# The opening of a fused attention-and-experts kernel: where the first bias column, two queries, the bias rows and the first probabilities are computed

## The chip, the cores and the metric

One core of a Trainium2 chip. The metric is the device time of one launch in microseconds (us), lower is better. The kernel before took 1143.11 us, the median of three runs.

## What is computed

Eight sequences of 512 tokens with 512 channels go through a two-way cross-attention with a gate, a residual, and a layer of 8 experts of which each token takes one. Cut to what matters here:

```python
def xattn(char_emb, subword_emb, ...):            # char_emb = layernorm(x), subword_emb = ctx_1024
    Q_char, K_sub, V_sub = linear(char_emb, Wq_c, bq_c), linear(subword_emb, Wk_s, bk_s), linear(subword_emb, Wv_s, bv_s)
    char2sub = softmax(Q_char @ K_sub.T * scale) @ V_sub
    Q_sub, K_char, V_char = linear(subword_emb, Wq_s, bq_s), linear(char_emb, Wk_c, bk_c), linear(char_emb, Wv_c, bv_c)
    sub2char = softmax(Q_sub @ K_char.T * scale) @ V_char
    gate = sigmoid(concat([char2sub, sub2char]) @ Wg.T + bg)
    return gate * char2sub + (1 - gate) * sub2char
x = x + tanh(g_xattn) * xattn(layernorm(x), ctx_1024, ...)
x = x + tanh(g_ffn) * (gate * expert_of_the_token(layernorm(x)))
```

## The kernel before, in words

**Products.** Every 512-wide product is done in two halves of each operand (a rounded high half on fp32r, and the rest): `product` (L155) issues 12 matmuls, 4 chunks of the contraction by 3 pairs of halves. After it ScalarE copies the bank out as the high half (`hi`), and VectorE subtracts that from the bank to give the low half (`lo`). So each 128x512 tile costs a ScalarE and a VectorE instruction, and the tensor engine (PE) waits for `lo`.

**The folded weights.** A query and a key product are replaced by one: for each direction the kernel first computes A = Wq^T Wk. The steps AC and AD (L416, L435 to L438) do that for direction 0, chunk by chunk as the weights come in, into the four banks `u0` to `u3`; AE empties them. A10 to A13 are direction 1. The steps W are the two halves of the raw weights, W00 to W03 of direction 0 and W10 to W13 of direction 1. What the biases add is folded as well: a column of 4x128 numbers Wk^T b that is added to each query (`c_col`, from step FOLD0 for direction 0 and FOLD2 for direction 1), and a row of 512 numbers, with which each token of x or of the context is dotted (`u_row`, from FOLD1 and FOLD2; the dots are the steps XD and CD, L1361 and L1367). SC are VectorE's scaled sums of weight rows (L380) that FOLD1 and FOLD2 read; the sum over the partitions is a matmul with ones.

**Order of the work.** The order is a list of named steps, written by hand, the same list for all five engines; each engine does its own part of each step and skips steps in which it has none. `opening_steps` (L180) is followed by `steps_of_a_batch(True, False)` (L479) for the first sequence, then a hardware loop over sequences 1 to 6, then the last one and the experts. An engine's queue is in order, so an instruction that waits holds up everything behind it in the list. Names end in digits for direction and number (Q02: direction 0, tile 2), or in one digit where there is no direction.

**The steps around the change.** XS (L1343) takes mean and variance of 128 rows of x on VectorE, and GpSimd (L1489) raises the variance to the power -1/2. XN (L1356) normalises the rows; for the first sequence on VectorE, for all later ones on ScalarE (L1211). XT (L1091) transposes them on PE and gives the moving operand of the queries. Q (L1024) is the query product, S (L1038) the scores, NP and S on VectorE the softmax (L1273: reciprocal of the sum, then the rows times it), V the values, PT the transposed probabilities, U the attended values, CT the halves of the context columns, AH and AL the emptying of A10 to A13's banks, WT, WH and WL the halves of the late weights, SM the small scalars, BC the constants of the biases.

**Banks.** `mm0` and `mm1` alternate over the steps Q, V, S and G (`Banks.take`, L793, and `take`, L993); `tr0` and `tr1` take transposes and FOLD1 and FOLD2. FOLD0 writes its column to `mm0`: 4 column tiles by 4 chunks, 16 matmuls with one moving column each, which read the raw fp32 weights and so run as 32 instructions. Queries wait for it:

```python
elif kind == "FOLD":
    if i == 0:
        pe.wait_ge(b_ready, 1)
        for m in range(C):
            for c in range(C):
                last = pe.matmul(column_bank[0][:, m:m + 1], raw[0][1][:, c, m * P:(m + 1) * P],
                                 column(0, 1, c), start=c == 0, stop=c == C - 1)
```

The order of the opening is:

```python
names = """WARM0 W00 AC00 W01 AC01 XS0 W02 XS1 XN0 XS2 W03 AC02 XN1 B0 XS3 XT0 XN2 AC03 XT1 XN3 AE00 AD03
           XT2 XT3 FOLD0 AE01 AE02 AE03 W10 BC0"""
```

GpSimd fills a constant (`fill_i`, L342) in its part of step FOLD2, without a wait. The split of the router's weights in three bf16 parts (L358) belongs to FOLD1 on VectorE.

Of the kernel before, what the change touches and what calls it, by code (L numbers as in the profile page):

```python
# [73 lines left out]
def gated_attention_and_experts(nc, x, ctx_in, g_xattn, g_ffn, Wq_c, bq_c, Wk_s, bk_s, bv_s,  # L74
# [10 lines left out]
    with ExitStack() as top:  # L85
# [26 lines left out]
        k.x1_tile = sb("x1_tile", [P, 2, H])  # L112
        k.junk = sb("junk", [P, H], BF16)
# [63 lines left out]
WEIGHTS_STEPS = ("WARM", "B", "BC", "W", "SC", "AC", "AD", "A", "AE", "AH", "AL", "FOLD", "SM")  # L177
# [14 lines left out]
def weights_part(nc, top, k, x1_dram, list_dram, w):  # L192
# [3 lines left out]
    column_bank = (k.mm_bank[0], k.tr_bank[1], k.tr_bank[1])  # L196
# [15 lines left out]
    in_parts = on_desk(3 * C * E).rearrange("p (n c e) -> p n c e", n=3, c=C)  # L212
# [16 lines left out]
    folded_up = sem("folded_up")  # L229
# [34 lines left out]
    def scalar(act):  # L264
# [7 lines left out]
        def run(step):  # L272
# [15 lines left out]
            elif kind == "SM":  # L288
                act.wait_ge(small_loaded, SMALL)
                act.activation(k.tanh_g[:], g_raw, ACT.Tanh).then_inc(scalars_ready, 1)  # L290
            elif kind in ("AE", "AH"):
                evicted[0] += 1
                if d == 1 and i == 0:
                    act.wait_ge(fold_read, 3)
                    act.wait_ge(router_split, 2 * PARTS - 1)
                act.wait_ge(group_mm, evicted[0])
                act.activation(arena[:, A_X + d, HI, i], bank[i][:], ACT.Copy).then_inc(group_hi, 1)
# [11 lines left out]
    def gpsimd(pool):  # L309
# [29 lines left out]
        def run(step):  # L339
            kind, _, d, c = step  # L340
            if kind == "FOLD" and c == 2:
# [7 lines left out]
    def vector(dve):  # L349
# [19 lines left out]
        def run(step):  # L369
            kind, _, d, i = step  # L370
            if kind == "BC":
# [4 lines left out]
                then(dve.reduce_sum(b_const, product_of, axis=AX))  # L376
            elif kind == "SM":
# [16 lines left out]
            elif kind == "FOLD":  # L394
                dve.wait_ge(fold_mm, i + 1)
                if i != 1:
                    ins = dve.tensor_copy(k.c_col[:, i // 2], column_bank[i][:, 0:C])
# [3 lines left out]
                if i != 0:  # L401
                    dve.tensor_scalar(k.u_const[:, i - 1:i], column_bank[i][:, C:C + 1], SCALE, None, ALU.mult)
                    ins = dve.tensor_copy(k.u_row[:, i - 1], row_bank[:])
                ins.then_inc(fold_read, 1)
                dve.wait_ge(fold_read, i + 1)
                if i == 1:
                    split_router()
# [7 lines left out]
    def tensor(pe):  # L415
# [13 lines left out]
        def run(step):  # L429
# [9 lines left out]
            elif kind == "A":  # L439
                if i == 0:  # L440
                    pe.wait_ge(nat_lo, 16)
                    pe.wait_ge(group_lo, C)
                product(pe, bank[i][:], lambda a, c: pair[1][0][:, a, c, i * P:(i + 1) * P],
                        lambda b, c: pair[1][1][:, b, c]).then_inc(group_mm, 1)
# [34 lines left out]
def steps_of_a_batch(first, last):  # L479
# [38 lines left out]
    s += late(4) + cur("U", 0, 0) + prev("BS", 3) + cur("PT", 0, 1) + opened("CD1")  # L518
# [69 lines left out]
def attention_part(nc, scope, top, k, x_rows, c_rows, x_columns, ctx_columns, x1_dram, x1_early, list_dram, expert_w,  # L588
# [6 lines left out]
    junk, bn_x, mv_x, x1_tile = k.junk, k.bn_x, k.mv_x, k.x1_tile  # L595

# [11 lines left out]
    diff = sb("diff", [P, H])  # L608
# [43 lines left out]
    q_lo, v_lo, u_lo, pt_lo, ct_lo, xt_lo = (sem(n) for n in ("q_lo", "v_lo", "u_lo", "pt_lo", "ct_lo", "xt_lo"))  # L652
    neg_top_ready, exp_done, probs_ready = sem("neg_top_ready"), sem("exp_done"), sem("probs_ready")
# [134 lines left out]
    class Banks:  # L788

        def __init__(self):  # L790
            self.n = 0

        def take(self, step):  # L793
# [9 lines left out]
            if kind not in IN_MM:  # L803
                return None
            self.n += 1
# [182 lines left out]
    def tensor(pe, weights_run, experts_run):  # L988
# [4 lines left out]
        def take(b, step, before_loop):  # L993

            if step[0] in IN_TR or step[0] == "LG":
                bank = tr_bank_of(step)
                name = "mm1" if bank is mm_bank[1] else "tr0" if bank is tr_bank[0] else "tr1"
            else:
# [16 lines left out]
        def run(b, steps):  # L1015
            here = turn[0]
            for step in steps:
# [6 lines left out]
                if kind == "Q":  # L1024
                    if i == 0 and d == 0:
                        pe.wait_ge(xt_lo, 4 * b + 4)
                        if here == 0:
                            pe.wait_ge(weights.fold_read, 1)
# [82 lines left out]
                elif kind in WEIGHTS_STEPS:  # L1111
                    weights_run(step)
# [28 lines left out]
    def scalar(act, weights_run, experts_run):  # L1141
        banks = Banks()
        run_weights, fill_lists, lists_filled = weights_run

        def run(b, steps, first=False):
            for kind, rel, d, i in steps:
# [11 lines left out]
                elif kind == "S":  # L1158
                    if d == 0 and i == 0 and not first:
# [3 lines left out]
                                   accum_out=p_sum[:, d, i:i + 1]).then_inc(exp_done, 1)  # L1163
                elif kind == "PT":
# [10 lines left out]
                elif kind == "KC":  # L1175
                    if i == 0:
                        act.wait_ge(u_lo, 8 * b + 4)
                        if first:
                            act.wait_ge(c_dotted, T)
                            lists_filled()  # L1180
                        else:
# [29 lines left out]
                elif kind == "XN" and not (first and rel == 0):  # L1211
# [36 lines left out]
        run(0, opening_steps() + steps_of_a_batch(True, False), first=True)  # L1248
        with act.Fori(1, B - 1) as b:
# [8 lines left out]
    def vector(dve, weights_run, experts_run):  # L1258
# [14 lines left out]
        def normalise_rows(b, d, i):  # L1273
            dve.wait_ge(exp_done, per_dir(b, d, i))
            then(dve.reciprocal(p_sum[:, d, i:i + 1], p_sum[:, d, i:i + 1]))
# [8 lines left out]
        def run(b, steps, here_first=False):  # L1284
            for kind, rel, d, i in steps:
# [8 lines left out]
                elif kind == "S":  # L1294
                    if d == 0 and i == 0:
                        dve.wait_ge(x_dotted, 4 * b + 4)
                        if not here_first:
                            dve.wait_ge(c_dotted, 4 * b + 4)
                        of = slice(0, 1 if here_first else 2)
# [609 lines left out]
```

## Time and profile before

| | before |
|---|---|
| median of three runs | 1143.11 us |
| lowest, highest | 1138.18, 1143.3 us |
| time of the profiled execution | 1138.43 us |
| its span | 1136.7 us |
| PE busy | 1116.7 us, 98% |
| VectorE (DVE), ScalarE (ACT), GpSimd (POOL) busy | 710.0, 440.4, 198.6 us |
| mean granted TensorE clock | 0.992 |

Times inside the trace count from the start of the span. A matmul's end is modelled, so starts are the better guide; "idle before" in square brackets is the time an engine stood still before an instruction, with what ended it. The opening, before the first score product, is the first 54 us.

### The profile page before, as it was taken

To read this page: it belongs to the slowest core of one execution; us is meant where nothing else is said; L and a number is where in the kernel's file an instruction comes from. 1 tells how busy PE (TensorE), PEld (TensorE's weight loads), DVE (VectorE), ACT (ScalarE), POOL (GpSimd) and SP (SyncE) were. 2 spreads that over 40 slices of the span, in tenths; PEclk is the share of its full clock that TensorE was granted. 3 is DMA by queue.
4 is the path that set the end of the run, shared out by engine and by line. 5 is a ranking of instruction groups with operands and counts; after the bars stand their busy time and mean duration, and the time that the engine had idled before them with its cause. 6 is when DMAs were issued, how large, how long until landed. Compare 5 with 4: busy or idle time off the path is not lost.

```text
span 1136.7 us, 17321 instructions
## 1 busy us (share of the span) xinstructions
PE 1116.7 (98%) x5639; PEld 918.7 (81%) x5639; DVE 710.0 (62%) x1496; ACT 440.4 (39%) x799; POOL 198.6 (17%) x322
## 2 busy tenths in 40 slices
PE   8999999999999999999999999999999999988998
PEld 7778888888888888888888888888888888777786
DVE  5866756565646564665576456645665656877665
ACT  4344524342434243433343244423342444643342
POOL 2000101120102010210011001101110102167564
PEclk9999999999999999999999999999999999989999
DMA  8232211021102210211021002210210332676683
GB/s 299 76 114 89 72 32 66 22 67 65 74 18 68 65 74 10 76 65 62 12 81 70 37 37 67 66 55 37 57 58 9 112 101 67 212 239 190 193 260 111
DMA packets 63138, 99.00 MB, mean 87 GB/s; under 512 B 20122, under 2 KB 20662, under 8 KB 63096
## 3 DMA queue, kind: packets, MB, share of 16 engines
q1 hardware_dynamic: 52928, 72.64, 20.2%
q0 software_dynamic: 7264, 19.20, 5.2%
q10 hardware_dynamic: 2904, 6.63, 1.6%
q8 instruction: 22, 0.36, 0.1%
q14 instruction: 20, 0.16, 0.0%
HBM read 71.15 MB, written 29.12 MB: 88 GB/s over the span
## 4 chain that ended last, share of the span: by engine, by line
PE 92%; DVE 3%; issue 1%; DMA 1%; another core or an unknown queue 1%; ACT 1%; SPq 1%; POOL 0%; DVEq 0%; ACTq 0%; POOLq 0%
PE mm L162 60%; PE u L1062 15%; PE u L162 8%; PE tr L1012 5%; PE mm L1854 1%; PE tr L162 1%; PE tr L1106 1%; DVE arena L1281 1%; DMA x_rows<-diff 1%; DVE slot_as_f L386 1%; DMA pairs_as_f<-in_x 0%; PE mm L450 0%; DVE arena L392 0%; ACT pairs_as_f L1714 0%
## 5 line engine op out<-in xcount | busy, mean ns | idle before, releaser
L162 PE MATMUL mm<-arena 128*128 128x512 f32 x1536 | 368.8, 393 | 0.3 <-issue 0.3
L162 PEld LDWEIGHTS mm<-arena 128*128 128x128 f32 x1536 | 286.5, 189 | 59.1 <-issue 0.4
L1062 PE MATMUL u<-arena 128*128 128x512 f32 x768 | 188.8, 396 | 0.0
L162 PE MATMUL mm<-arena,q_pair 128*128 128x512 f32 x768 | 180.0, 392 | 0.3 <-issue 0.3
L162 PEld LDWEIGHTS mm<-arena,q_pair 128*128 128x128 f32 x768 | 142.5, 188 | 31.3 <-issue 1.1
L1062 PEld LDWEIGHTS u<-arena 128*128 128x128 f32 x768 | 140.6, 188 | 28.1 <-DVE arena L410 0.2
L1281 DVE TENSOR_TENSOR arena<-mm,arena 128x512 fp32r<-128x512 f32 x65 | 44.9, 691 | 99.1 <-ACT arena L1157 95.1
L1157 ACT ACTIVATE arena<-mm 128x512 fp32r<-128x512 f32 x64 | 38.2, 598 | 146.1 <-PE mm L162 146.1
L1153 ACT ACTIVATE q_pair<-mm,c_col 128x512 fp32r<-128x512 f32 x64 | 44.1, 689 | 123.1 <-PE mm L162 123.1
L1162 ACT ACTIVATE probs<-mm,neg_top 128x512 f32<-128x512 f32 x64 | 44.1, 689 | 118.6 <-DVE neg_top L1306 117.2
L162 PE MATMUL mm<-c2s_pair,arena 128*128 128x512 f32 x360 | 87.1, 391 | 0.0
L162 PE MATMUL mm<-q_pair,arena 128*128 128x512 f32 x360 | 86.4, 389 | 0.0
L1282 DVE SCALAR_TENSOR_TENSOR q_pair<-mm,c_col,q_pair 128x512 fp32r<-128x512 f32 x64 | 48.0, 750 | 55.2 <-ACT q_pair L1153 54.4
L162 PE MATMUL u<-arena,q_pair 128*128 x312 | 80.1, 407 | 0.0
L162 PEld LDWEIGHTS mm<-q_pair,arena 128*128 128x128 f32 x360 | 67.6, 188 | 14.0
L162 PEld LDWEIGHTS mm<-c2s_pair,arena 128*128 128x128 f32 x360 | 67.0, 188 | 13.7
L1477 POOL TENSOR_SCALAR mv_x<-mv_x 128x1 f32<-128x1 f32 x28 | 12.6, 450 | 371.7 <-DVE mv_x L1348 371.7
L1281 DVE TENSOR_TENSOR arena<-tr,arena 128x512 fp32r<-128x512 f32 x95 | 64.0, 686 | 15.3 <-ACT arena L1166 10.8
L1477 POOL TENSOR_SCALAR stats<-stats 128x1 f32<-128x1 f32 x32 | 7.5, 233 | 355.3 <-DVE stats L1391 355.1
L162 PEld LDWEIGHTS u<-arena,q_pair 128*128 128x128 f32 x312 | 58.4, 194 | 11.8
L1325 DVE SCALAR_TENSOR_TENSOR probs<-probs,u 128x512 f32<-128x512 f32 x32 | 21.9, 686 | 72.2 <-ACT probs L1192 72.1
L1192 ACT ACTIVATE probs<-mm,bg_half 128x512 f32<-128x512 f32 x30 | 20.7, 689 | 116.3 <-PE mm L162 116.3
(241 smaller groups left out, 1491.0 us busy)
## 6 DMA issues: line engine op xcount, KB each, us to landing
slot_as_f<-in_ctx_by_columns SPq DMA_DIRECT2D x8, 1024.0 KB, 5.6
in_tile<-in_ctx SPq DMA_DIRECT2D x31, 256.0 KB, 2.7
x_rows<-x_tile SPq DMA_DIRECT2D x30, 256.0 KB
in_tile<-in_x SPq DMA_DIRECT2D x28, 256.0 KB, 2.7
slot_as_f<-in_x_by_columns SPq DMA_DIRECT2D x7, 1024.0 KB, 5.2
x_rows_early<-x_tile SPq DMA_DIRECT2D x28, 256.0 KB, 2.3
probs<-in_L_ffn_expert_b SPq DMA_DIRECT2D x21, 256.0 KB
slot_as_f<-in_L_ffn_expert_w SPq DMA_DIRECT2D x4, 1024.0 KB, 5.5
```

Source lines behind the costliest of these rows:

```text
L162: last = pe.matmul(bank, lhsT(a, c), rhs(b, c), start=start and n == 0, stop=stop and n == C * len(PASSES) - 1)
L386: ins = dve.scalar_tensor_tensor(folded[d][n], raw[d][n][:, i], column(d, n, i), folded[d][n], ALU.mult, ALU.add)
L1012: last = pe.transpose(bank[:, tile(n)], block_of(n), ident[:])
L1062: last = pe.matmul(u_bank[m][:], v_pair[:, i % 2, a, tile(m)], pt_pair[:, i % 2, p], start=i == 0 and n == 0, stop=i == T - 1 and n == 2)
L1153: act.activation(q_pair[:, HI, i], bank[:], ACT.Identity, bias=c_col[:, d, i:i + 1]).then_inc(q_hi, 1)
L1157: act.activation(v_pair[:, i % 2, HI], bank[:], ACT.Copy).then_inc(v_hi, 1)
L1162: act.activation(probs[:, i], bank[:], ACT.Exp, bias=neg_top[:, d, i:i + 1], scale=SCALE, accum_out=p_sum[:, d, i:i + 1]).then_inc(exp_don ...
L1192: act.activation(probs[:, i], bank[:], ACT.Tanh, bias=bg_half[:, i:i + 1], scale=0.5).then_inc(tanh_done, 1)
L1281: return dve.tensor_tensor(to, bank, f32(hi), ALU.subtract)
L1282: return dve.scalar_tensor_tensor(to, bank, bias, f32(hi), ALU.add, ALU.subtract)
L1325: dve.scalar_tensor_tensor(mix, mix, 1.0, u_bank[i][:], ALU.subtract, ALU.mult).then_inc(nd_used, 1)
L1477: then(pool.tensor_scalar(rstd, var, EPS, None, ALU.add))
```

## The change

- **FOLD0.** VectorE builds the scaled sum of the four chunks of Wk_s (new step ACC, four instructions, after AE03 and around W10) and PE sums it over the partitions by 4 matmuls with ones (8 instructions), into bank `u3`, after Q01. The copy to `c_col` is a new step FR on VectorE, between W11 and W12.
- **Queries.** The wait of Q00 for the bias column is gone from PE. Q00 and Q01 stand before FOLD0, and Q02 and Q03 use `tr0` and `tr1`. FOLD1 waits on PE for Q03's low half. The steps W11, FR0, SM0, W12 and W13 stand before Q00 in the list.
- **XN0, XN1, XN2** of the first sequence go from VectorE to ScalarE, with a second small instruction each on GpSimd (L1493) for the bias; XN3 stays on VectorE and stands ahead of XT1.
- **Bias rows.** The copies of FOLD1 and FOLD2 into `u_row` go to ScalarE; VectorE waits for them. The router's split becomes a step SR0, after CD1. The router's raw weights lie in `diff`.
- **First probabilities.** For direction 0 of the first sequence ScalarE multiplies the rows by the reciprocal sum; VectorE does only the reciprocal.
- **Dots.** XD0 is after WT1; XD1, XD2 and XD3 stand between the scores S00 to S03, and write `row_const` directly. The copy of L1300 goes for the first sequence.
- **GpSimd's fill** is in FOLD1, behind a wait for the direction 0 products.

```diff
-    names = """WARM0 W00 AC00 W01 AC01 XS0 W02 XS1 XN0 XS2 W03 AC02 XN1 B0 XS3 XT0 XN2 AC03 XT1 XN3 AE00 AD03
-               XT2 XT3 FOLD0 AE01 AE02 AE03 W10 BC0"""
+    names = """WARM0 W00 AC00 W01 AC01 XS0 W02 XS1 XN0 XS2 W03 AC02 XN1 B0 XS3 XT0 XN2 AC03 XN3 XT1 AE00 AD03
+               XT2 XT3 AE01 AE02 AE03 ACC00 ACC01 W10 ACC02 ACC03 BC0"""
...
-        names = """Q00 W11 SM0 Q01 W12 Q02 W13 SC00 SC01 Q03 SC02 SC03 A10 SC10 WT0 A11 SC11 SC12 FOLD1 SC13 XD0 CT0 A12
-                   CT1 WT1 CT2 A13 CT3 XD1 FOLD2 XD2 XD3 AH10 AH11 AL10 S00
-                   AL11 WH2 S01 WL2 WH3 S02 WL3 S03 NP03"""
+        names = """W11 FR0 SM0 W12 W13 Q00 Q01 FOLD0 Q02 Q03 SC00 SC01 SC02 SC03 A10 SC10 WT0 A11 SC11 SC12 FOLD1 SC13
+                   CT0 A12 CT1 CT2 A13 CT3 WT1 XD0 FOLD2 AH10 AH11 AL10 S00
+                   XD1 AL11 WH2 S01 XD2 WL2 WH3 S02 XD3 WL3 S03 NP03"""
...
+            elif kind == "ACC":
+                if i == 0:
+                    dve.wait_ge(b_ready, 1)
+                    ins = dve.tensor_scalar(folded[0][1], raw[0][1][:, i], column(0, 1, i), None, ALU.mult)
+                else:
+                    dve.wait_ge(folded_col, i)
+                    ins = dve.scalar_tensor_tensor(folded[0][1], raw[0][1][:, i], column(0, 1, i), folded[0][1],
+                                                   ALU.mult, ALU.add)
+                ins.then_inc(folded_col, 1)
+            elif kind == "FR":
+                dve.wait_ge(fold_mm, 1)
+                dve.tensor_copy(k.c_col[:, 0], column_bank[0][:, 0:C]).then_inc(fold_read, 1)
...
                 if i == 0:
-                    pe.wait_ge(b_ready, 1)
+                    pe.wait_ge(folded_col, C)
+                    pe.wait_ge(group_lo, C)
                     for m in range(C):
-                        for c in range(C):
-                            last = pe.matmul(column_bank[0][:, m:m + 1], raw[0][1][:, c, m * P:(m + 1) * P],
-                                             column(0, 1, c), start=c == 0, stop=c == C - 1)
+                        last = pe.matmul(column_bank[0][:, m:m + 1], folded[0][1][:, m * P:(m + 1) * P], ones[:, 0:1],
+                                         start=True, stop=True)
...
+            elif kind == "FOLD" and i > 0:
+                act.wait_ge(fold_mm, i + 1)
+                act.activation(k.u_row[:, i - 1], row_bank[:], ACT.Copy).then_inc(fold_read, 1)
...
-                        if here == 0:
-                            pe.wait_ge(weights.fold_read, 1)
...
+            if self.first and kind == "Q" and d == 0 and i > 1:
+                return tr_bank[i - 2]
...
+        def normalise_rows(i):
+            act.wait_ge(sums_inverted, i + 1)
+            act.activation(probs[:, i], probs[:, i], ACT.Copy, scale=p_sum[:, 0, i:i + 1]).then_inc(probs_ready, 1)
...
-                elif kind == "XN" and not (first and rel == 0):
+                elif kind == "XN" and not (first and rel == 0 and i == T - 1):
...
-                        pool.tensor_tensor(stat[:, 2:3], stat[:, 2:3], minus_half[:], ALU.pow).then_inc(x_scaled, 1)
+                        ins = pool.tensor_tensor(stat[:, 2:3], stat[:, 2:3], minus_half[:], ALU.pow)
+                        if i < T - 1:
+                            then(ins)
+                            ins = pool.tensor_scalar(stat[:, 1:2], stat[:, 0:1], stat[:, 2:3], -1.0, ALU.mult, ALU.mult)
+                        ins.then_inc(x_scaled, 1)
```

## Rows read from the trace of the kernel before

**Rows 1.** The page: busy time by engine, and engines' shares of the chain.

```profile
PE 1116.7 (98%) x5639; PEld 918.7 (81%) x5639; DVE 710.0 (62%) x1496; ACT 440.4 (39%) x799; POOL 198.6 (17%) x322
...
PE 92%; DVE 3%; issue 1%; DMA 1%; another core or an unknown queue 1%; ACT 1%; SPq 1%; POOL 0%; DVEq 0%; ACTq 0%; POOLq 0%
```

**Rows 2.** Timeline of PE, 17 to 69 us: start, duration, line, operands, count.

```profile
17.29 1.64 PE L424 MATMUL u<-arena 128*128 128x512 f32 x6
...
21.33 4.98 PE L450 MATMUL mm<-slot_as_f 128*128 128x1 f32 x32
26.61 12.83 PE L162 MATMUL mm<-arena 128*128 128x512 f32 x48 [0.30 <-issue]
39.49 5.74 PE L162 MATMUL u<-arena 128*128 128x512 f32 x24
...
51.86 0.95 PE L458 MATMUL tr<-slot_as_f 128*128 128x1 f32 x8
...
54.27 11.55 PE L162 MATMUL mm<-arena,q_pair 128*128 128x512 f32 x48 [0.28 <-issue]
65.66 2.88 PE L162 MATMUL mm<-arena 128*128 128x512 f32 x12
68.61 0.63 PE L1012 MATMUL tr<-ident,probs 128*128 128x128 f32 x4
```

**Rows 3.** The chain that ended last, in a later, gapless stretch: start, duration.

```profile
142.97 24.54 PE mm L162 x108
```

**Rows 4.** Windows, all engines: PE, PEld, DVE, ACT, POOL, clock, DMA share, GB/s.

```profile
20.00:30.00 10.00, 9.37 (x48) 8.40 (x48) 6.15 (x13) 3.69 (x7) 0.00 (x0) 0.67 0.91 294
```

**Rows 5.** Windows of half a microsecond, PE alone: PE, clock, DMA share, GB/s.

```profile
30.00:30.50 0.50, 0.50 (x3) 0.83 1.01 393
```

**Rows 6.** Timeline of VectorE, 13 to 65 us.

```profile
13.77 0.69 DVE L1347 BATCH_NORM_STATS2 bn_x<-pairs_as_f 128x6 f32<-128x512 f32 x1
...
15.01 1.29 DVE L392 TENSOR_TENSOR arena<-slot_as_f,arena 128x512 fp32r<-128x512 f32 x2
...
18.54 1.20 DVE L1359 TENSOR_SCALAR pairs_as_f<-pairs_as_f,slot_as_f 128x512 f32<-128x512 f32 x1
...
20.25 0.53 DVE L1359 TENSOR_SCALAR pairs_as_f<-pairs_as_f,slot_as_f 128x512 f32<-128x512 f32 x1
...
22.16 0.69 DVE L1281 TENSOR_TENSOR arena<-mm,arena 128x512 fp32r<-128x512 f32 x1 [0.18 <-ACT arena L1196]
...
26.54 1.89 DVE L410 TENSOR_TENSOR arena<-u,arena 128x512 fp32r<-128x512 f32 x3
...
41.20 1.53 DVE L386 SCALAR_TENSOR_TENSOR slot_as_f<-slot_as_f 128x512 f32<-128x512 f32 x2
...
54.09 0.74 DVE L1363 CUSTOM_DVE_ANT_0 junk<-pairs_as_f,u_row,u_const 128x512 bf16<-128x512 f32 x1
...
64.32 0.49 DVE L1276 TENSOR_SCALAR probs<-probs,p_sum 128x512 f32<-128x512 f32 x1
64.72 0.68 DVE L1281 TENSOR_TENSOR arena<-slot_as_f,arena 128x512 fp32r<-128x512 f32 x1
```

**Rows 7.** Timeline of ScalarE, 22 to 67 us.

```profile
22.02 1.57 ACT L297 ACTIVATE arena<-u 128x512 fp32r<-128x512 f32 x3
...
66.97 0.69 ACT L1162 ACTIVATE probs<-mm,neg_top 128x512 f32<-128x512 f32 x1 [1.94 <-DVE neg_top L1306]
```

**Rows 8.** Timeline of GpSimd, 15 to 19 us.

```profile
15.16 0.95 POOL L1493 TENSOR_TENSOR slot_as_f<-slot_as_f,minus_half 128x1 f32<-128x1 f32 x1 [0.89 <-DVE slot_as_f L1352]
...
18.57 0.89 POOL L342 MEMSET x_tile<- 128x944 int32 x1
```

**Rows 9.** Groups by line over the span: busy us, mean ns | idle before, releaser.

```profile
L1214 ACT ACTIVATE in_tile<-in_tile,mv_x 128x512 f32<-128x512 f32 x28 | 22.6, 809 | 14.8 <-POOL mv_x L1479 14.8
...
L1479 POOL TENSOR_SCALAR mv_x<-mv_x 128x1 f32<-128x1 f32 x28 | 7.4, 265 | 5.9 <-POOL mv_x L1478 5.9
```

**Rows 10.** DMA issues, 0 to 60 us: KB each, median us to landing.

```profile
x_rows<-slot_as_f SPq DMA_DIRECT2D x1, 2.1 KB, 5.7
```

More of the change, by code:

```diff
@@ L340, in run @@
             kind, _, d, c = step
-            if kind == "FOLD" and c == 2:
+            if kind == "FOLD" and c == 1:
+                pool.wait_ge(group_mm, C)
                 pool.memset(fill_i, N).then_inc(filled, 1)
@@ L400, in run @@
                     then(dve.scalar_tensor_tensor(router_sb, sums, -1.0 / H, router_sb, ALU.mult, ALU.add))
[L401 to L404, printed above, removed]
+                else:
+                    then(dve.tensor_copy(k.c_col[:, 1], column_bank[i][:, 0:C]))
+                then(dve.tensor_scalar(k.u_const[:, i - 1:i], column_bank[i][:, C:C + 1], SCALE, None, ALU.mult))
                 dve.wait_ge(fold_read, i + 1)
-                if i == 1:
-                    split_router()
+            elif kind == "SR":
+                split_router()
             elif kind in ("AE", "AL"):
@@ L517, in steps_of_a_batch @@
     s += load(0)
-    s += late(4) + cur("U", 0, 0) + prev("BS", 3) + cur("PT", 0, 1) + opened("CD1")
+    s += late(4) + cur("U", 0, 0) + prev("BS", 3) + cur("PT", 0, 1) + opened("CD1 SR0")
     s += prev("LG", 2) + cur("V", 0, 2) + prev("NR", 3) + cur("PT", 0, 2) + opened("CD2") + late(5) + load(1)
@@ L790, in __init__ @@
         def __init__(self):
-            self.n = 0
+            self.n, self.first = 0, True
         def take(self, step):
@@ L997, in take @@
                 name = "mm1" if bank is mm_bank[1] else "tr0" if bank is tr_bank[0] else "tr1"
+            elif before_loop == 0 and step[0] == "Q" and step[2] == 0 and step[3] > 1:
+                name, bank = f"tr{step[3] - 2}", tr_bank[step[3] - 2]
             else:
@@ L1111, in run @@
                 elif kind in WEIGHTS_STEPS:
+                    if kind == "FOLD" and i == 1:
+                        pe.wait_ge(q_lo, per_dir(0, 0, 3))
                     weights_run(step)
@@ L1163, in run @@
                                    accum_out=p_sum[:, d, i:i + 1]).then_inc(exp_done, 1)
+                    if first and d == 0 and i > 0:
+                        normalise_rows(i - 1)
+                elif kind == "NP" and first and d == 0:
+                    normalise_rows(i)
                 elif kind == "PT":
@@ L1248, in scalar @@
         run(0, opening_steps() + steps_of_a_batch(True, False), first=True)
+        banks.first = False
         with act.Fori(1, B - 1) as b:
@@ L1271, in bn_ready, with normalise_rows @@
             dve.sem_inc(waits_passed_dve, 1)
-        def normalise_rows(b, d, i):
+        def normalise_rows(b, d, i, here_first):
             dve.wait_ge(exp_done, per_dir(b, d, i))
+            if here_first and d == 0:
+                dve.reciprocal(p_sum[:, d, i:i + 1], p_sum[:, d, i:i + 1]).then_inc(sums_inverted, 1)
+                return
             then(dve.reciprocal(p_sum[:, d, i:i + 1], p_sum[:, d, i:i + 1]))
@@ L1294, in run @@
                 elif kind == "S":
-                    if d == 0 and i == 0:
+                    if d == 0 and i == 0 and not here_first:
                         dve.wait_ge(x_dotted, 4 * b + 4)
-                        if not here_first:
-                            dve.wait_ge(c_dotted, 4 * b + 4)
-                        of = slice(0, 1 if here_first else 2)
-                        then(dve.tensor_copy(row_const[:, of], row_next[:, of]))
+                        dve.wait_ge(c_dotted, 4 * b + 4)
+                        then(dve.tensor_copy(row_const[:], row_next[:]))
                     dve.wait_ge(s_mm, per_dir(b, d, i))
@@ L1355, in run @@
                     dve.wait_ge(x_stats, per_batch(bb, i))
-                elif kind == "XN" and here_first and rel == 0:
+                elif kind == "XN" and here_first and rel == 0 and i == T - 1:
                     dve.wait_ge(x_scaled, per_batch(bb, i))
+                    dve.wait_ge(x_normed, T - 1)
                     rows, stat = x_of(bb, i), x_stat_of(bb, i)
@@ L1450, in vector @@
         run(0, opening_steps() + steps_of_a_batch(True, False), here_first=True)
+        banks.first = False
         done = chain["n"]
```

27 lines of the change are left out of this document (15 added, 12 removed).

## The prediction

> **What bounds the kernel now.** I read the page first: PE is busy 98% of the span and holds 92% of the chain that ended last [rows 1]. So a change on another engine pays only where it closes a gap on PE, takes work off PE, or gives it a better clock. Next I read PE's timeline of the opening [rows 2]: from 26.61 us on the starts follow each other with idle times of 0.3 us at most, so what stands before 26.61 us is the place to look. There the last 128x512 products (the second part of AC03) begin at 17.29 us and take 1.64 us; then only transposes and FOLD0 follow: 32 instructions with one moving column, from 21.33 us, 4.98 us. Queries begin at 26.61 us.
>
> The windows show what that stretch costs beyond itself: the mean granted clock from 20 to 30 us is 0.67 [rows 4], which is 6.6 us at 1.2 GHz in place of 2.4, and in the half microsecond from 30.0 it is 0.83 [rows 5], so the clock came back at about 30.17 us. The four queries take from 26.61 to 39.49 us, 12.88 us for 48 matmuls [rows 2]. Later in the kernel 108 matmuls take 24.54 us, 0.227 each [rows 3], and 48 would take 10.91: the queries lose 2.0 us to the clock.
>
> Last I read VectorE and ScalarE over the same stretch, since the order of the step list makes PE wait for their halves.
>
> **Step 1: when Q00 can start.** With FOLD0 out of the way Q00 needs the low half of XT3. It ended at 22.16 + 0.69 = 22.85 us [rows 6], and VectorE stood still only 0.18 us ahead of it. Off VectorE's queue go XN0 (0.5), XN1 (0.5) and XN2, which took 1.20 beside GpSimd's fill against 0.53 for XN3 [rows 6, 8]; 2.1 us in all. But XN3 now waits for GpSimd. From the row of XS2: it starts at 13.77, now 0.5 earlier at 13.27, and an XS step takes 15.01 - 13.77 = 1.24. So XS2 ends at 14.5, the two lows of W03 (1.24 of pitch) at 15.75, XS3 at 17.0; GpSimd's power takes up to 0.95 [rows 8], so XN3 runs from 18.0 to 18.5, where VectorE has stood some 0.4. Then the lows of XT1, AE00, XT2 and XT3 at 0.6 each: 21.0 us.
>
> Does ScalarE keep up? Its normalisation with two per-row operands takes 0.81, and the second GpSimd instruction 0.27 with 0.21 (5.9 / 28) ahead of it [rows 9]. XN2: 14.5 + 0.2 + 0.95 + 0.5 + 0.81 = 17.0 us, and PE wants it at about 18.0, after AD03. W03's high halves now stand behind XN0 on ScalarE and end near 14.3 us, before VectorE comes to them at 14.5. What is late next is XN3's statistics, not ScalarE. Bounds for Q00: 20.75 us (22.85 less 2.1) to 21.6 (XN3 beside the fill, below). I take 21.0: 5.6 us earlier than 26.61.
>
> **Step 2: Q00 to A10.** AE01 to AE03 follow XT3 on VectorE at 0.63 each (1.89 for three [rows 6]), at 21.6, 22.2 and 22.9 us. Q00's chunks of 0.68 want them at 21.7, 22.4 and 23.0: no wait. Q00 and Q01 end at 26.45. The new sum on VectorE: 0.45, then three at 0.67 (two SC steps took 1.53 with their tail [rows 6]), with W10's two lows (1.2) between: from 22.85 it ends at 26.5, with Q01. So ACC costs PE nothing; without that cover, up to 2.5 us. FOLD0's new form is 8 instructions, priced by the same form in FOLD2: 0.95 us [rows 2]. Q02 starts at 27.4 and Q03 ends at 32.9. They need no wait, since `tr0` and `tr1` are free, while the queue of evictions stands until FR0. VectorE comes to FR0 after BC0 and W11 (0.35 + 1.2), at 28.1; behind it are SM0, W12 and W13 (2.6) and then the queries' lows, and A10 waits for W13: 30.8 us, 2 us before PE wants it. ScalarE's eviction of Q00 waits for FR0 too, with Q01's and WT0 behind it; PE wants none of them before FOLD1, and Q03's low half, which FOLD1 waits for, comes at 34.3. SM0 now stands ahead of W12 on ScalarE: its last transfer was issued at 15.0 us and landed 5.7 later [rows 10], before ScalarE is there at 23.6. A10 starts at 32.9, not 39.49: **6.6 us**. It is 5.6 for the earlier start and 2.0 for the clock, less 0.95 for the new FOLD0.
>
> **Step 3: A10 to S00.** PE's work is the same, 54.27 - 39.49 = 14.78 us, so S00 can start at 47.7. VectorE: Q03's low 34.3, SC00 to SC03 2.4, SC10 0.85, WT0 0.6, SC11 and SC12 2.7, FOLD1 0.35, SC13 1.35, ScalarE's first context half 0.65, four lows 2.4: 45.6 us. FOLD1 and FOLD2 are two small writes each less, with ScalarE's copy (about 0.6) now waited for; behind that wait stand SC13 and AL10, neither late. The margin is 2.1 us. The dots and router split that leave here (3 x 0.82 [rows 6] and about 1.2 us) are what keeps that margin; on PE they are worth nothing by themselves.
>
> **Step 4: the scores.** S00 to V00 took 11.39 us for four products [rows 2] against 10.91 at the steady pitch. The excess is S02's wait for the bank that S00's exponential empties, behind two dots and the copy. With XD0 alone ahead, that is gone: -0.4 us. On VectorE each score step swaps the 0.40 pitch of the scaling (64.32 to 64.72) for a dot of 0.82. From the end of one score product to the last low of that step then takes about 2.65 us, and a product takes 2.73: it just fits. V00 waits for WL3 in that place.
>
> **Step 5: probabilities.** PT00 needs all four row tiles. Before, it came 1.64 us after the last exponential's start (68.61 - 66.97 [rows 2, 7]). Now ScalarE runs two scalings behind that exponential, the row of S02 and the row of S03. The trace has no copy with a per-row scale; the nearest rows are 0.69 with one such operand [rows 7] and 0.81 with two [rows 9]. I take 0.69, with a pitch of 0.6: 0.68 + 0.6 + 0.69 + 0.1 = 2.05. PT00 comes **+0.4** later (0.3 to 0.7). Its cover, V00, is already used up.
>
> **Other moves at nothing.** SR0 (1.2 us) on VectorE lies where it stood idle for over 1 us per product pair. The load of Wg's second half waits for FR0, 1.7 us later, and is used after 65 us. GpSimd's fill now starts at the end of AD03, 18.1 us, and nothing is queued behind it.
>
> **Sum.** -6.6 - 0.4 + 0.4 = -6.6 us. From V00 on nothing waits on a fixed date, as loads too are released by steps that moved, so the shift stays to the end. The profiled execution took 1138.43; it would be 1131.8. It was 4.7 us below the median of the runs, 1143.11, by which I forecast **1136.5 us**. A measurement of this kernel tells about 0.5%, 5.7 us, from no change, so this is just over the bound.
>
> **A rule against step 1.** XN2 took 1.20 us when it began 0.03 us ahead of GpSimd's fill, which took 0.89 [rows 6, 8]. The Trainium skill (SBUF — State Buffer, section "SBUF: two separate sides") says that VectorE and GpSimd share one pair of ports under an exclusive lock for a whole instruction. By that rule the change has not removed the clash, since the fill now starts at 18.1 beside XN3 (18.0 to 18.5), and the sum would be -6.0; by the rows alone, where only a start in the same moment is shown, it is -6.6. This goes into the range.
>
> **Rivals.**
> - *The clock falls all the same.* From 18.1 to 21.0 us PE has only the transposes of XT2 and XT3, and then Q00. Before, it fell at about 23.4 us (6.6 us before 30.0), 4.5 us after the last wide product. If it falls again, the queries lose the same 2.0 us: gain 4.6, 1138.5. For it: the stretch is as empty; against it: it is 2.9 us and was 7.7. The Trainium skill (TensorE: Matmul & The Clock Gate, "Part 1: The HAM clock gate") has half rate as the default that activity lifts, which would make this rival's fall possible. 17 in 100.
> - *VectorE becomes the bound.* The margins of 2 us at A10 and at S00 and of nothing at V00 are thin; XN3 beside the fill and a late ACC or WL3 would give back 2 us: gain 4.5, 1138.6. 13 in 100.
> - *The shift is lost,* or the change does not reach PE, because a later step waits for something that does not move: 1142. Against it: no idle time over 0.3 us on PE. 7 in 100.
> - *Slower: the clock stays at half through the queries.* Place: Q00 to A10, paced chunk by chunk by AE01 to AE03. Price: each product costs another 2.73 us; beyond 2.4 products the gain is gone, and if all four queries and A10 run so, 5 x 2.73 = 13.65 us against 6.6: 1150.2. Against it: the clock came back 3.6 us after the products began [rows 2, 5]. 4 in 100.
>
> The forecast has 54 in 100, and a gain over 8 us 5. Over 5.7 us faster: 54, 5 and a part of the rest: 0.61; slower by as much 0.04; the remaining 0.35 within. The range, 1130.5 to 1141.5, goes from a gain of 8 us, with the run to run spread that put two runs of three 5 us above the lowest, to one of 2 us and holds the first two rivals.
>
> **What would show it.** Q00's first matmul near 21 us; FOLD0 with 8 instructions of 0.95 us between Q01 and Q02; a granted clock of 1.00 from 20 to 30 us; A10 near 33, S00 near 47.7, V00 near 58.6; 0.4 us of idle PE before PT00. I am wrong if the 20 to 30 us window is below 0.9, if A10 or S00 has a gap ended by VectorE, or if the shift at V00 is 7 us and the end's is not.

## The result, and the profile after

Fifteen runs of each kernel gave medians of 1134.22 us against 1139.69 us, 5.5 us less. The ratio that is worked out from all of the runs is 0.9942, with a 95% interval of 0.993 to 0.9954: 6.6 us less, between 5.2 and 8.0. The first three runs of before, which the prediction had, gave 1143.11, 3.4 us above the median of fifteen. So the forecast time, 1136.5, is 2.3 us too high, while the forecast gain agrees.

The profiled execution of the changed kernel took 1135.31 us, with a span of 1133.6. The page, busy time and chain by engine [rows 1]:

```profile
PE 1110.6 (98%) x5615; PEld 913.7 (81%) x5615; DVE 707.2 (62%) x1490; ACT 445.7 (39%) x808; POOL 201.7 (18%) x325
...
PE 94%; issue 2%; ACT 1%; DVE 1%; another core or an unknown queue 1%; DMA 1%; POOL 0%; SPq 0%; ACTq 0%; POOLq 0%; DVEq 0%
```

PE is as much the bound as it was. Its timeline, 17 to 62 us, with the starts that answer to [rows 2]:

```profile
17.08 1.64 PE L437 MATMUL u<-arena 128*128 128x512 f32 x6
...
21.16 5.78 PE L163 MATMUL mm<-arena 128*128 128x512 f32 x24 [1.57 <-DVE arena L1314]
26.79 1.05 PE L465 MATMUL u<-slot_as_f 128*128 128x1 f32 x8
27.70 5.75 PE L163 MATMUL tr<-arena 128*128 128x512 f32 x24
33.29 5.60 PE L163 MATMUL u<-arena 128*128 128x512 f32 x24
...
45.52 0.94 PE L473 MATMUL tr<-slot_as_f 128*128 128x1 f32 x8
...
47.09 11.47 PE L163 MATMUL mm<-arena,q_pair 128*128 128x512 f32 x48
58.56 3.00 PE L163 MATMUL mm<-arena 128*128 128x512 f32 x12
61.85 0.63 PE L1032 MATMUL tr<-ident,probs 128*128 128x128 f32 x4 [0.29 <-ACT probs L1167]
```

And the window from 20 to 30 us (PE, PEld, DVE, ACT, POOL, granted clock, DMA share, GB/s), where the clock had been 0.67 [rows 4]:

```profile
20.00:30.00 10.00, 8.84 (x42) 7.23 (x43) 9.86 (x20) 7.25 (x15) 0.00 (x0) 1.00 0.67 243
```

The starts of both kernels in us, with how much earlier they came than before:

| | before | after | earlier | forecast |
|---|---|---|---|---|
| Q00 | 26.61 | 21.16 | 5.45 | 5.6 |
| A10 | 39.49 | 33.29 | 6.20 | 6.6 |
| S00 | 54.27 | 47.09 | 7.18 | 6.6 |
| V00 | 65.66 | 58.56 | 7.10 | 7.0 |
| PT00 | 68.61 | 61.85 | 6.76 | 6.6 |
| first transpose of the expert stage | 985.15 | 978.12 | 7.03 | 6.6 |

A small part of this is not the change. The first statistics of x (XS0, when its rows have landed) began at 9.61 us before and at 9.26 after. In a second profile of the changed kernel, further down, XS0 began at 9.96 and Q00 at 21.44: 5.17 us earlier than before, with the later input.

The last line of the table is 916 us behind PT00: PE's timeline at that place in the two kernels, before and after,

```profile
985.15 0.60 PE L1854 MATMUL mm<-ident,pairs_as_f 128*128 128x128 f32 x4
```

```profile
978.12 0.60 PE L1892 MATMUL mm<-ident,pairs_as_f 128*128 128x128 f32 x4
```

So nothing is lost in the sequences between. The spans, though, differ by only 3.1 us, 1136.7 to 1133.6: from that transpose to the end the profiled executions took 151.6 us before and 155.5 after. That part was not touched; below is what other runs show of it.

### The profile page after: what moved, and what is told of

It reads as the page before. It is cut to its first block, busy times and chain, and to the rows that moved or that the text cites. A ratio compares the mean times of both kernels' runs of the same rounds, so it can differ in the third digit from the quotient of the medians.

```text
span 1133.6 us, 17283 instructions
## 1 busy us (share of the span) xinstructions
PE 1110.6 (98%) x5615; PEld 913.7 (81%) x5615; DVE 707.2 (62%) x1490; ACT 445.7 (39%) x808; POOL 201.7 (18%) x325
## 4 chain that ended last, share of the span: by engine, by line
PE 94%; issue 2%; ACT 1%; DVE 1%; another core or an unknown queue 1%; DMA 1%; POOL 0%; SPq 0%; ACTq 0%; POOLq 0%; DVEq 0%
PE mm L163 59%; PE u L1080 16%; PE u L163 9%; PE tr L1032 5%; PE mm L1892 2%; PE tr L163 1%; PE u L437 1%; PE tr L1124 1%; DMA x_rows<-diff 1%; ACT pairs_as_f L1752 0%; PE mm L483 0%; DVE arena L1314 0%; DVE mx L1333 0%; PE tr L1140 0%
## 5 line engine op out<-in xcount | busy, mean ns | idle before, releaser
L163 PE MATMUL mm<-arena 128*128 128x512 f32 x1512 | 361.6, 392 | 1.6 <-DVE arena L1314 1.6
L163 PEld LDWEIGHTS mm<-arena 128*128 128x128 f32 x1512 | 280.8, 188 | 59.2 <-DVE arena L1314 1.8
```

The costliest lines, as they stand in the source:

```text
L163: last = pe.matmul(bank, lhsT(a, c), rhs(b, c), start=start and n == 0, stop=stop and n == C * len(PASSES) - 1)
```

## The experiments

All start from the changed kernel. They were run in three groups, each on another chip, on which the kernel before had medians of 1142.59 (one run), 1132.96 (nine runs) and 1141.2 us (eleven runs). Most edits were run once, so their effect is read in the trace, as the start of a named product, and not in the time of the run. The date at which the first rows of x land differs between executions: XS0 began between 9.24 and 10.65 us in the fourteen profiles. A later date moves Q00 by as much only where VectorE's queue is what Q00 waits for. In the changed kernel VectorE has a wait of 0.54 us on the way, and an input 0.70 us later moved Q00 by only 0.28. A table of all profiles stands at the end of this section.

### FOLD0 in its old form at the new place

```diff
-                        last = pe.matmul(column_bank[0][:, m:m + 1], folded[0][1][:, m * P:(m + 1) * P], ones[:, 0:1],
-                                         start=True, stop=True)
+                        for c in range(C):
+                            last = pe.matmul(column_bank[0][:, m:m + 1], raw[0][1][:, c, m * P:(m + 1) * P],
+                                             column(0, 1, c), start=c == 0, stop=c == C - 1)
```

The four ACC steps are taken out of the list as well.

> The changed kernel, with FOLD0 in its old form (16 matmuls with one moving column on the raw weights) at its new place after Q01, and without VectorE's sum. In the kernel before, FOLD0's first 22 of 32 instructions took 2.85 us at 2.4 GHz, so 32 take about 3.7 us, against 0.9 for the new form. If the form is worth its PE time alone: Q02 starts 2.8 us later than the 27.70 us of the changed kernel, and A10, S00 and V00 are later by the same (A10 36.1, V00 61.4), with the granted clock at 1.00, since wide products stand on both sides. If the rival holds, that such a run of narrow matmuls lowers the clock wherever it stands, the clock falls to half during or after it and A10 is 4 to 5 us later.

The rival in this expectation held. PE's timeline:

```profile
21.44 5.75 PE L163 MATMUL mm<-arena 128*128 128x512 f32 x24 [1.57 <-DVE arena L1315]
27.02 3.63 PE L466 MATMUL u<-slot_as_f 128*128 128x1 f32 x32
30.51 7.30 PE L163 MATMUL tr<-arena 128*128 128x512 f32 x24
37.65 5.60 PE L163 MATMUL u<-arena 128*128 128x512 f32 x24
```

and its windows (PE busy, clock, DMA share, GB/s):

```profile
28.00:30.00 2.00, 2.00 (x20) 1.00 0.02 8
30.00:32.00 2.00, 2.00 (x10) 0.66 0.11 4
32.00:34.00 2.00, 2.00 (x7) 0.50 0.89 227
34.00:36.00 2.00, 2.00 (x10) 0.99 0.76 293
```

PE counts as busy without a gap, and the clock still fell, just after 3.5 us of matmuls with one moving column. From Q00's start A10 came 16.21 us later, against 12.13 in the changed kernel: 4.1 us, of which 2.6 are the 32 instructions (27.02 to 30.51, against 0.91) and 1.5 the two queries at half clock. Against the kernel before (39.49) A10 is 1.8 us earlier with the place alone, and 6.2 with place and form. The Trainium skill (TensorE: Matmul & The Clock Gate, "Part 1: The HAM clock gate") has the clock follow how busy PE has been. By the profile's busy time this trace does not agree: PE was busy without a gap from 22 us on, and the clock fell.

### FOLD0 in its new form, ahead of Q00

```diff
-        names = """W11 FR0 SM0 W12 W13 Q00 Q01 FOLD0 Q02 Q03 SC00 ...
+        names = """FOLD0 W11 FR0 SM0 W12 W13 Q00 Q01 Q02 Q03 SC00 ...
```

> The changed kernel, with FOLD0 in its new form but ahead of Q00, as before: PE waits for the last ACC at 26.7 us. By the sum: Q00 starts at 27.7, after 8 us with only transposes; the clock falls as in the kernel before, near 23 us, and the queries lose 1.5 to 2 us; A10 at 27.7 + 10.9 + 2 = 40.5 us, 7 us later than the changed kernel's 33.29, so the whole gain at A10 comes from the place and none of it from the form. By the rival in which the one-column matmuls brought the clock down, it stays at 1.00 here and A10 starts at 38.7.

PE stood still 7.2 us, and the clock fell at about 22.5 us with no narrow matmul ahead of it (mean 0.63 from 22 to 24 us), and came back near 32.8. The timeline:

```profile
26.18 1.87 PE L465 MATMUL u<-slot_as_f 128*128 128x1 f32 x8 [7.20 <-DVE slot_as_f L387]
27.91 8.01 PE L163 MATMUL mm<-arena 128*128 128x512 f32 x24
35.76 5.60 PE L163 MATMUL tr<-arena 128*128 128x512 f32 x24
41.20 5.60 PE L163 MATMUL u<-arena 128*128 128x512 f32 x24
```

A10 at 41.20 us is 7.9 later than in the changed kernel and 1.7 later than before. VectorE's sum is free only because Q00 and Q01 run beside it. So place and form do not add up. Against the kernel before, and with the rest of the change always there, A10 gains 1.8 us with the new place alone, loses 1.7 with the new form alone, and gains 6.2 with both. The expectation that none of the gain at A10 comes from the form is contradicted by the run above. The clock fell behind one-column matmuls there and behind idle time here; in the kernel before, PE had some of each ahead of the fall at 23.4 us, and how much each did there is not shown.

### Normalisation back on VectorE

```diff
-                elif kind == "XN" and not (first and rel == 0 and i == T - 1):
+                elif kind == "XN" and not (first and rel == 0):
...
-                elif kind == "XN" and here_first and rel == 0 and i == T - 1:
+                elif kind == "XN" and here_first and rel == 0:
...
-                        if i < T - 1:
+                        if False:
```

> The changed kernel, with the first three normalisations back on VectorE (and GpSimd's second instruction gone). If VectorE's queue sets Q00's start, three instructions of 0.5 us come back to it, less the 0.54 us that it now waits for ScalarE before XT2: Q00 starts 0.8 to 1.5 us later than 21.16, at 22.0 to 22.7, and A10 as much, while the clock stays at 1.00. If ScalarE's chain (GpSimd's power, second instruction, 0.81 us) is what sets it, Q00 starts at 21.2 or earlier. If the emptier stretch brings the clock down, the queries take 1 to 2 us more on top.

Q00 at 22.74 us, A10 at 34.86, the clock at 1.00. VectorE's chain began 0.38 us later in this run (XS1 at 12.10, against 11.72), and here it had no wait between, so 1.2 us are the edit's, as expected. Two normalisations in a row took 1.72 us in it, where one takes 0.55, since GpSimd's fill ran beside them.

### GpSimd's fill without its wait

```diff
-                pool.wait_ge(group_mm, C)
```

> The changed kernel, with GpSimd's fill without its wait, so that it starts right after the last power, near 17.4 us, beside XN3 on VectorE (17.41 us, 0.55 us long). If two engines share a pair of ports with a lock, the one that begins second waits for the other: XN3 takes 1.1 to 1.4 us, XT3's low half and Q00 are 0.5 to 0.8 us later (Q00 at 21.7 to 22.0). If the 1.20 us of XN2 in the kernel before had another cause, XN3 stays at 0.55 and Q00 at 21.16.

VectorE's timeline, and GpSimd's:

```profile
18.79 1.08 DVE L1390 TENSOR_SCALAR pairs_as_f<-pairs_as_f,slot_as_f 128x512 f32<-128x512 f32 x1
```

```profile
18.70 0.89 POOL L345 MEMSET x_tile<- 128x944 int32 x1
```

XN3 took 1.08 us; in the changed kernel it took 0.55, and the fill came only at 18.77, beside AE00's low half, which reads PSUM and took its usual 0.68. So the clash is real, with 0.53 us of waiting, and the new wait avoids it. The Trainium skill (SBUF — State Buffer, "SBUF: two separate sides") has it as an exclusive lock, which whichever starts first gets for the whole instruction. The traces agree in part: the fill kept its 0.89 us, and the normalisation ended 0.28 us after the fill's end, here as in the kernel before. But there XN2 had begun 0.03 us ahead of the fill [rows 6, 8] and was held all the same, so that the first to begin wins is not shown. What it costs Q00 is not settled: Q00 started at 22.31, but in this run VectorE's chain was 1.4 us late from its inputs on.

### Q02 and Q03 in the matmul banks

```diff
-            if self.first and kind == "Q" and d == 0 and i > 1:
-                return tr_bank[i - 2]
```

with the same taken out of PE's choice of banks.

> The changed kernel, with Q02 and Q03 in the two matmul banks, as before. Q02 then waits for the low half of Q00, which stands on VectorE behind FR0, W12 and W13 and ended at 31.5 us: Q02 starts at 31.6 in place of 27.70, Q03 follows, and A10 starts at 37.1, 3.8 us later. A gap of 3.9 us without any matmul may bring the clock down: then A10 is at 38 to 39. If the transpose banks are worth nothing (Q00's low half is drained in time), Q02 starts at 27.7.

```profile
31.73 7.95 PE L163 MATMUL mm<-arena 128*128 128x512 f32 x24 [3.80 <-DVE q_pair L1311]
39.51 5.60 PE L163 MATMUL u<-arena 128*128 128x512 f32 x24
```

PE's timeline shows it: Q02 waited 3.8 us for Q00's low half, the clock fell near 29.6 us and both queries ran at half for most of their time: A10 6.2 us later, the whole gain at that place. The wait itself is 3.9 of it, the clock 2.2; my expectation had the wait right and the clock too low.

### VectorE's later relief undone

The copies of the bias rows and the router's split go back to VectorE's FOLD steps, and the dots ahead of S00:

```diff
-                   CT0 A12 CT1 CT2 A13 CT3 WT1 XD0 FOLD2 AH10 AH11 AL10 S00
-                   XD1 AL11 WH2 S01 XD2 WL2 WH3 S02 XD3 WL3 S03 NP03"""
+                   XD0 CT0 A12 CT1 CT2 A13 CT3 WT1 XD1 FOLD2 XD2 XD3 AH10 AH11 AL10 S00
+                   AL11 WH2 S01 WL2 WH3 S02 WL3 S03 NP03"""
```

> The changed kernel, with all of VectorE's later relief undone: the bias rows copied by VectorE, the router's split back in FOLD1, and the dots XD0 to XD3 ahead of S00. The queries stay as changed. In the changed kernel the last context low half ends at 46.7 us and S00 starts at 47.09, a margin of 0.4 us. Ahead of that low half come back 0.6 (u_row), 1.2 (split) and 0.8 (XD0): 2.6 us. If the relief is what lets PE use its earlier start, A10 stays at 33.3 and S00 starts 1.5 to 2.5 us later, near 49.1, and S02 and the softmax are later by up to 1 us more. If it is worth nothing on PE, S00 stays at 47.1 and V00 at 58.6.

```profile
33.52 5.60 PE L163 MATMUL u<-arena 128*128 128x512 f32 x24
...
49.00 5.72 PE L163 MATMUL mm<-arena,q_pair 128*128 128x512 f32 x24 [1.12 <-issue]
55.45 5.76 PE L163 MATMUL mm<-arena,q_pair 128*128 128x512 f32 x24 [0.73 <-ACT probs L1186]
61.05 2.88 PE L163 MATMUL mm<-arena 128*128 128x512 f32 x12
64.51 0.63 PE L1032 MATMUL tr<-ident,probs 128*128 128x128 f32 x4 [0.58 <-ACT probs L1167]
```

From A10 to S00 15.48 us against 13.80, to V00 27.53 against 25.27, to PT00 30.99 against 28.56: the relief is worth 2.4 us. The same 2.4 us stand at the first transpose of the expert stage (947.23 us after A10, against 944.83). Three edits were undone together, so which of them carries the 2.4 us is not shown. Note the first wait: it is put down to "issue", but S00 waits there for the last context low half on VectorE, whose timeline has them as one group of five:

```profile
46.40 3.10 DVE L1314 TENSOR_TENSOR arena<-slot_as_f,arena 128x512 fp32r<-128x512 f32 x5 [0.18 <-ACT arena L1232]
```

By the order of the steps the context's four come first and WT1's is the fifth, so the last of the four ends at 48.9 us, 0.1 ahead of S00.

### Who scales the first probabilities

All four rows back on VectorE (both helpers restored):

> The changed kernel, with the first probabilities scaled on VectorE, as before. In the changed kernel PT00 starts 2.14 us after the last exponential's start (59.71 to 61.85), before it was 1.64 us. If ScalarE's two scalings in a row are the cost, PT00 follows V00 without a gap, 0.3 to 0.5 us earlier against V00's start. But on VectorE each score step is then 0.4 us longer, and WL3's low half, which V00 waits for, may come later: V00's start moves from 11.47 us after S00 to 11.5 to 12.2 us. Sum at PT00, against S00: between -0.4 and +0.4 us. If the scaling's engine does not matter, both stay.

```profile
46.95 11.47 PE L163 MATMUL mm<-arena,q_pair 128*128 128x512 f32 x48
59.22 2.98 PE L163 MATMUL mm<-arena 128*128 128x512 f32 x12 [0.80 <-DVE arena L1307]
62.04 0.60 PE L1032 MATMUL tr<-ident,probs 128*128 128x128 f32 x4
```

V00 waits 0.80 us for WL3's low half, and PT00 comes 15.09 us after S00, against 14.76: the move to ScalarE gains 0.33 us in sum, a little past the longest V00 delay that I had expected.

Only the last row on VectorE:

```diff
-            if here_first and d == 0:
+            if here_first and d == 0 and i < T - 1:
```

> The changed kernel, with the last of the four rows of the first probabilities scaled on VectorE and the other three on ScalarE. The two engines then work side by side: VectorE's reciprocal at 0.81 us after the exponential's start, its scaling 0.5 behind; ScalarE's scaling of the third row ends at 1.4. PT00 starts 1.6 us after the exponential in place of 2.14, and the gap of 0.29 us on PE ahead of PT00 is gone; V00's start stays. Gain 0.3 to 0.5 us on the changed kernel, 0.9935 to 0.9945 of the kernel before: within the spread of the runs, to be read in the trace.

PT00 came 14.29 us after S00, 0.47 earlier, but U00 only 0.32 earlier (64.82), and the expert stage's first transpose 0.06 (930.97 us after S00, against 931.03). The gap moved behind V01: AE13's low half ended at 64.77 us, just ahead of U00. By five runs the ratio to the kernel before is 0.9928 (0.9915 to 0.9942); the changed kernel itself was not run in this group.

Then also AE12 ahead of S00:

> The kernel with the last row scaled on VectorE, where PT00 came 0.47 us earlier against S00 but U00 only 0.32, since VectorE still had AE13's low half to do (it ended at 64.77, U00 began at 64.82). Here AE12 (emptying of bank u2) also goes ahead of S00 on ScalarE, with its low half behind XD1, so VectorE has one instruction of 0.6 us less between V00 and U00. If that queue is what U00 waits for, U00 starts 17.4 us after S00, against 17.66 there and 17.98 in the changed kernel. If the queue in the scores is too full for it, V00 starts later than 11.47 us after S00.

U00 17.48 us after S00, V00 11.47; the expert stage 930.56, so 0.47 us better than the changed kernel. The edit above pays at the far end only with this one; whether this one pays without it was not tried.

### Transposes ahead of AD03, and all three edits

```diff
-    ... XN2 AC03 XN3 XT1 AE00 AD03
-               XT2 XT3 AE01 AE02 AE03 ACC00 ...
+    ... XN2 AC03 XN3 XT1 XT2 XT3
+               AE00 AD03 AE01 AE02 AE03 ACC00 ...
```

> The changed kernel, with the transposes XT2 and XT3 (and their two halves) ahead of AE00 and AD03. In the changed kernel PE did AD03 (17.08 to 18.55 us) before XT2, ScalarE had XT2's bank at 19.18, and PE then stood still 1.57 us until VectorE's low half. If the order of the steps sets Q00, XT2 can start at 17.4 and XT3 at 18.0, the lows of XT1, XT2, XT3 and AE00 follow each other from 18.0 at 0.6 each, and Q00 starts at 20.5, A10 at 32.7, both 0.6 us earlier, with the clock at 1.00. If XN3 and the lows behind it set it in any order, Q00 stays at 21.1. GpSimd's fill then starts near 19.9 beside VectorE instructions that read PSUM, and should cost nothing.

Q00 at 20.77 us with VectorE's chain at the same date as in the changed kernel (XS2 at 12.95 and 12.96): 0.4 us earlier, not 0.6. XT2 waited 0.34 us for `tr0`, which XT0's low half still held.

> The changed kernel with the three edits together: the last row of the first probabilities on VectorE, AE12 ahead of S00, and XT2 and XT3 ahead of AE00 and AD03. Sum of the parts: U00 1.1 to 1.2 us earlier than in the changed kernel (65.07), near 63.9, and the first transpose of the expert stage near 977.0 in place of 978.12. Against the kernel before that is 7.7 to 8.2 us of about 1135, a ratio of 0.9925 to 0.9935; the changed kernel itself is at 0.994.

> The changed kernel as it is, on the same chip as the three others. Up to the expert stage it should repeat itself within 0.3 us (Q00 near 21.2, A10 33.3, S00 47.1, the stage's first transpose at 978.1), wherever it runs; what differs from run to run and from chip to chip should lie behind that, in the expert stage, which took 151.6 us in the profiled run of the kernel before and 155.5 in that of the changed one. Against the kernel before: 0.994, between 0.993 and 0.995.

The three edits together: Q00 at 21.23, U00 64.54 and the expert stage at 977.70, in a run whose XS2 was 0.47 us late. VectorE has no such wait any more in this order of steps: against the run with the transposes alone XS2 was 0.48 us later and Q00 0.46. So with the input at the date of the changed kernel's first profile, an estimate from these starts is a gain of 0.9 us on it, not 1.1 to 1.2. As read it is 0.4 us on the first profile (978.12) and 0.7 on the second (978.38). By six runs each its ratio is 0.9926 (0.9909 to 0.9943) and that of the changed kernel 0.9931 (0.991 to 0.9951): both beat the kernel before, and by these times the two can't be told apart. The changed kernel repeated itself up to the expert stage (21.44, 33.57, 47.37 and 978.38 us), and the stage itself took 152.1 us, where it had taken 155.5. Over all fourteen profiles the stage took 151.1 to 155.5 us in ten, and 144.3 to 145.8 in the four of the second group, where the kernel before too was 8 us faster. The spread there is larger than all that this change does, so the gain shows in many runs taken together and in starts ahead of the stage.

All fourteen profiles, in us; the last column is from the stage's first transpose to the end of the span:

| kernel | group | XS0 | A10 | first transpose of the expert stage | stage |
|---|---|---|---|---|---|
| before | | 9.61 | 39.49 | 985.15 | 151.6 |
| changed | | 9.26 | 33.29 | 978.12 | 155.5 |
| changed, second profile | 3 | 9.96 | 33.57 | 978.38 | 152.1 |
| old form of FOLD0 | 1 | 10.13 | 37.65 | 982.49 | 154.1 |
| FOLD0 ahead of Q00 | 1 | 9.24 | 41.20 | 986.04 | 154.0 |
| normalisation on VectorE | 1 | 9.64 | 34.86 | 979.68 | 153.5 |
| two banks | 1 | 9.94 | 39.51 | 984.36 | 151.1 |
| fill without its wait | 2 | 10.65 | 34.41 | 979.25 | 145.6 |
| relief undone | 2 | 9.37 | 33.52 | 980.75 | 145.8 |
| all four rows on VectorE | 2 | 9.71 | 33.15 | 978.65 | 144.3 |
| last row on VectorE | 2 | 9.31 | 33.36 | 978.13 | 144.5 |
| and AE12 ahead of S00 | 3 | 9.41 | 33.01 | 977.37 | 154.9 |
| transposes first | 3 | 9.25 | 32.79 | 977.57 | 154.8 |
| all three | 3 | 9.72 | 33.26 | 977.70 | 155.4 |

What an edit of FOLD0, of the normalisations or of the banks did to A10 is still there, within 0.1 us, 945 us later.

## Why the prediction was right

The forecast of 6.6 us is met by the ratio (5.5 by the medians), and the start of the expert stage came 7.0 us earlier. That the sum came out so closely is in part luck, since its terms missed in opposite directions: A10 gave 6.2 in place of 6.6, S00 some 0.5 in place of nothing, the scores 0.24 in place of 0.4, PT00 cost 0.34 in place of 0.4, and 0.14 came between A10 and FOLD2; that makes 6.76 at PT00.

- **Step 1** held: Q00 at 21.16, forecast 21.0. VectorE's list ran as added up, 0.3 us ahead of it (XS2 at 12.96, forecast 13.27) as the input was, but the wait was in another place: XN3 began at 17.41, not 18.0, since GpSimd's last power took 0.55 us, and then VectorE waited 0.54 us for ScalarE's half of XT2, behind AD03. Normalisations on ScalarE took 0.81, as priced.
- **The rule against step 1** gave the wrong date, not the wrong mechanism: XN3 was over at 17.96 and the fill began at 18.77.
- **Step 2** held: the clock stayed at 1.00, FOLD0 took 0.91 us, A10 came at 33.29. FOLD0 began at 26.79, forecast 26.45, but ACC was not the cause: from Q00 to FOLD0 were 5.63 us, and 5.58 in the run without ACC. That the queries needed wide products around FOLD0 and also its short form, I had not said: I counted the form only by its own 4.3 us.
- **Step 3 was mis-sized.** "The margin is 2.1 us", and the relief "worth nothing by themselves" on PE. The margin was 0.3. VectorE's timeline of after has the four context lows and WT1's as

```profile
44.28 3.10 DVE L1314 TENSOR_TENSOR arena<-slot_as_f,arena 128x512 fp32r<-128x512 f32 x5 [0.78 <-ACT arena L1232]
```

  so the context's last ended at 46.78 us, and S00 began at 47.09. And the kernel before had waited there: VectorE's timeline of before has its five lows as

```profile
51.07 3.10 DVE L1281 TENSOR_TENSOR arena<-slot_as_f,arena 128x512 fp32r<-128x512 f32 x5 [0.18 <-ACT arena L1203]
```

  which end at 54.17 us, the context's last among them, and S00 began at 54.27. I had read PE's waits by who ended them, and this one stood under "issue" with 0.28 us [rows 2]. The start of S00 makes the gain look larger than it is (from FOLD2's start 2.41 us before [rows 2], 1.57 after), because after the change its first matmul is recorded while FOLD2's last one still runs. Its second matmul is the better mark, PE's timeline before and after:

```profile
54.58 0.63 PE L162 MATMUL mm<-arena,q_pair 128*128 128x512 f32 x2
```

```profile
47.72 0.62 PE L163 MATMUL mm<-arena,q_pair 128*128 128x512 f32 x2
```

  From FOLD2's start that is 2.72 us before and 2.20 after: 0.5 us gained that I had put at nothing. At the new pace the relief is worth 2.4 us.
- **Step 4 had the wait right and its worth too large.** From S00 to V00 were 11.47 us, not 11.0, and 11.39 before. But S02's wait for the bank was there and is gone. The weight loads of the tensor engine (PEld) show it, before and then after:

```profile
60.06 5.33 PEld L162 LDWEIGHTS mm<-arena,q_pair 128*128 128x128 f32 x24 [0.49 <-ACT probs L1162]
```

```profile
47.49 10.64 PEld L163 LDWEIGHTS mm<-arena,q_pair 128*128 128x128 f32 x47 [0.24 <-issue]
58.53 0.53 PEld L163 LDWEIGHTS mm<-arena 128*128 128x128 f32 x3 [0.40 <-issue]
```

  Counted from S00's second matmul, V00 came 11.08 us later before and 10.84 after: 0.24 of the 0.4 us. The rest went into a new wait of about 0.16 us at V00, listed as "issue", right behind WL3's low half, which ended at 58.41 (57.72 and 0.69). So the dots between the scores did not quite fit; with one scaling more per step V00 waits 0.8 us.
- **Step 5** held: PT00 is 0.34 us later against V00, forecast 0.4; a copy with a per-row scale takes 0.71 us.
- Of the **rivals**, the fallen clock did not come, but lies near: 7.2 us of standing still, 3.5 us of narrow matmuls, or a wait of 3.8 us behind the 0.9 us of FOLD0 brought it. VectorE as the bound is what the kernel would have met without its relief. Nothing of the shift was lost.

## What to carry to other kernels

In this kernel 3.5 us of matmuls with one moving column were followed by half clock, though the profile counts them as busy: let VectorE add up over the chunks and keep one matmul per column tile, between wide products, and read the granted clock behind every stretch of narrow matmuls. When work is pulled forward by several microseconds, look at each margin on the helper engines again, and compare the end of the last producer with the consumer's start yourself, since a wait for several semaphores may be listed as "issue". Where two engines share a chain of small steps, closing one gap shows the next: price the edit at the far end, not at the gap.

## What the runs showed of the hardware beyond that

The expert stage, the same code in every run, took 144.3 to 155.5 us, and the four short values are the four profiles of the second group; no profile of another group is below 151. Of the 20 us from 1040 to 1060 PE was busy 19.2 to 20.0 in those four and 15.2 to 16.9 in the other ten. Since each group had a chip of its own, the chip may be the cause, but this was not tried. The clock stayed at half for 3.4 us in the run with the old form, 6.8 in the one without the two banks and in the kernel before, and about 10 us where PE had stood still for 7.2 us.
